# Attention on one core: transposes of the probabilities in pairs of units, with the value products behind them

## The reference

```python
scores = jnp.einsum('bsgqd,btgd->bgqst', q, k) * scale
scores = jnp.where(causal, scores, jnp.finfo(scores.dtype).min)
attn = jax.nn.softmax(scores, axis=-1)
out = jnp.einsum('bgqst,btgd->bsgqd', attn, v)
```

## Time and profile before

| | |
|---|---|
| median of the runs | 927.78 us |
| the profiled execution's time | 926.08 us |
| its span | 924.3 us |
| TensorE (PE) busy | 909.6 us, 98% |
| weight loads (PEld) busy | 804.3 us, 87% |
| VectorE (DVE) busy | 628.5 us, 68% |
| ScalarE (ACT) busy | 514.9 us, 56% |
| GpSimd (POOL) busy | 488.1 us, 53% |
| granted TensorE clock | 1.00 |

### The profile page before, as it was taken

The page is one execution under the profiler, slowest core; times in us unless marked ns, Lnnn a source line. Parts: engine busy times, 40 slices in busy tenths (PEclk is TensorE's granted clock), DMA queues, the critical chain, the costliest instruction groups (busy, mean ns, idle before and its releaser), DMA issues.

```text
span 924.3 us, 15010 instructions
## 1 busy us (share of the span) xinstructions
PE 909.6 (98%) x5480; PEld 804.3 (87%) x5480; DVE 628.5 (68%) x1297; ACT 514.9 (56%) x1121; POOL 488.1 (53%) x699
## 2 busy tenths in 40 slices
PE   6999999999999999999999999999999999999997
PEld 5889889888888898888888898888888998888886
DVE  6578668856786678647875787378757876764554
ACT  4376566745765566557664766476647667531111
POOL 1386638561866286708671867076717989410000
PEclk9999999999999999999999999999999999999999
DMA  8000100000001000000010000000001001000000
GB/s 284 1 24 1 40 1 24 1 29 1 24 1 40 1 23 1 29 1 23 2 41 1 24 1 29 2 1 24 1 1 69 1 14 62 1 23 0 23 23 23
DMA packets 10180, 21.21 MB, mean 23 GB/s; under 512 B 1280, under 2 KB 5760, under 8 KB 9984
## 3 DMA queue, kind: packets, MB, share of 16 engines
q1 hardware_dynamic: 9392, 20.11, 6.4%
q10 hardware_dynamic: 720, 0.21, 0.1%
HBM read 18.22 MB, written 2.10 MB: 22 GB/s over the span
## 4 chain that ended last, share of the span: by engine, by line
PE 94%; DVE 2%; ACT 2%; issue 1%; DMA 0%; SPq 0%; DVEq 0%; ACTq 0%
PE ps L1286 13%; PE ps L1129 13%; PE ps L1130 13%; PE ps L1131 13%; PE ps L1307 7%; PE ps L1304 7%; PE ps L1305 7%; PE ps L1269 7%; PE ps L1275 6%; PE ps L1272 6%; ACT prob L780 1%; PE ps L1153 1%; DVE ps L1042 1%; PE ps L1140 1%; PE ps L1265 1%
## 5 line engine op out<-in xcount | busy, mean ns | idle before, releaser
L625 POOL TENSOR_TENSOR rinv<-rsum,mone 128x1 f32<-128x1 f32 x256 | 140.9, 550 | 230.5 <-ACT prob L780 229.9
L1046 DVE TENSOR_TENSOR pt_lo<-ps,pt_hi 128x512 fp32r<-128x512 f32 x288 | 198.1, 688 | 64.6 <-ACT pt_hi L804 61.3
L804 ACT ACTIVATE pt_hi<-ps 128x512 fp32r<-128x512 f32 x288 | 171.2, 597 | 116.5 <-PE ps L1286 114.2
L780 ACT ACTIVATE prob<-ps,nmax 128x256 f32<-128x256 f32 (+28 forms) x256 | 180.7, 706 | 82.9 <-DVE nmax L1042 81.1
L630 POOL TENSOR_SCALAR prob<-prob,rinv 128x256 f32<-128x256 f32 (+28 forms) x256 | 190.2, 743 | 38.8 <-POOL rinv L625 38.5
L1042 DVE CUSTOM_DVE_ANT_0 ps<-ps,mask_f 128x256 f32<-128x256 f32 (+28 forms) x256 | 183.1, 718 | 38.6 <-PE ps L1275 33.0
L1286 PE MATMUL ps<-ident,prob 128*128 128x128 f32 x1152 | 172.6, 273 | 1.0 <-POOL prob L630 0.8
L1286 PEld LDWEIGHTS ps<-ident,prob 128*128 128x128 f32 x1152 | 140.4, 141 | 20.9 <-DVE pt_lo L1046 3.4
L1304 PE MATMUL ps<-pt_hi,v_hi 128*128 128x512 f32 x288 | 134.3, 466 | 0.0
L1307 PE MATMUL ps<-pt_lo,v_hi 128*128 128x512 f32 x288 | 114.1, 396 | 0.0
L1305 PE MATMUL ps<-pt_hi,v_lo 128*128 128x512 f32 x288 | 113.5, 394 | 0.0
(11 more groups left out here) (179 smaller groups left out, 1814.1 us busy)
## 6 DMA issues: line engine op xcount, KB each, us to landing
w_raw<-in_wqkv SPq DMA_DIRECT2D x8, 640.0 KB, 4.1
wp_raw<-in_wproj SPq DMA_DIRECT2D x8, 512.0 KB, 3.5
out_y<-prob SPq DMA_DIRECT2D x8, 256.0 KB, 2.3
x<-in_x SPq DMA_DIRECT2D x3, 512.0 KB, 12.2
prob<-in_wug SPq DMA_DIRECT2D x3, 512.0 KB, 4.1
prob<-in_wmod SPq DMA_DIRECT2D x1, 1024.0 KB, 9.6
wv_raw<-in_wv SPq DMA_DIRECT2D x4, 256.0 KB, 4.6
raw_down<-in_wdn SPq DMA_DIRECT2D x1, 1024.0 KB, 4.8
```

The costliest lines, as they stand in the source:

```text
L780: a_.activation(row(i, h).rearrange("p (a n) -> p a n", a=nb), score_banks(i, h).rearrange("p (a n) -> p a n", a=nb)[:, :, 0:w], ACT.Exp, ...
L1046: v_.tensor_tensor(pt_lo[:, n % 3, :], ring(t, "T", n), pt_hi[:, n % 3, :].bitcast(F32), ALU.subtract).then_inc(ptl_done, 1)
```

## The change

A function `together` rewrites the list after it is made. For each n of 4, 6, 8, ... up to 34 (in the last turn up to 26) it puts T(n-1), T(n), V(n-3), V(n-2) at the place of T(n-1), and all that stood between them behind, in its old order. ScalarE's copy `pt_hi` of units above 2 gets a wait for V(n-3), which reads the same slot.

```diff
-WALK = walk()
+def together(order):
+    for t in range(TURNS):
+        for n in range(4, NU if t + 1 < TURNS else LAST[WINDOWS[2][0]] + 1, 2):
+            first = order.index((t, "T", n - 1, 0))
+            stop = order.index((t, "V", n - 2, 0)) + 1
+            pair = [(t, "T", n - 1, 0), (t, "T", n, 0), (t, "V", n - 3, 0), (t, "V", n - 2, 0)]
+            rest = [item for item in order[first:stop] if item not in pair]
+            order[first:stop] = pair + rest
+    return order
+
+WALK = together(walk())
...
                 if what == "T":
                     act.wait_ge(t_done, this(t_done, t, n + 1))
+                    if n > 2:
+                        act.wait_ge(pv_done, this(pv_done, t, n - 2))
                     a_.activation(pt_hi[:, n % 3, :], ring(t, "T", n), ACT.Copy).then_inc(pth_done, 1)
```

## The result

The kernel after takes 963.35 us (median of five runs, 961.22 to 966.54), the kernel before beside it on the same chip 927.44 us (926.73 to 928.13): ratio 1.0393, 95% interval 1.038 to 1.0406. Forecast were 963 us and a range of 943 to 980. The profiled execution took 963.04 us with a span of 961.3 us, 37.0 us more than that of before. The five runs differ in their mean granted clock: the fastest, 961.22 us, has 1.000, the profiled one 0.998, and the three slowest 0.995.

What follows compares the result with a forecast made beforehand. TensorE was taken as the bound, with almost no gaps, and grouping as saving nothing. A 8, B 5, C 14 and D 8.4 make 35 us on the profiled 926.1, so 961; the median's 1.7 more gives 963, range 943 to 980.

Steps and rivals of the forecast that it cites:

- B: S5.3, each turn: waits for an exponential whose maximum stands behind LF; 0.6 us a turn, 5 us over eight turns.
- C: T15 and T16, each turn: T16 waits 1.6 us for the modulation; 1.75 us a turn, 14 us over eight turns.
- A: T4 and T6, each turn: they wait for pt_lo, 0.47 and 0.78 us; 8 us over eight turns.
- D: End of seven turns: S0.1 waits 0.8 us for S7.3's exponential; with smaller waits 1.2 us a turn, 8.4 us.
- rival 6: Around T16: the clock falls and T13 to V14 take up to twice as long; 56 us more, 1019 us; chance 0.02.
- Rival 2: All pairs: changing from transposes to products costs 0.09 us, which grouping saves, and waits are hidden; 917 us; chance 0.05.
- rival 3: All turns: the waits appear, but long steps behind them take each up; about 928 us, no change; chance 0.04.
- 4: All turns: only part of the waits appears, as ScalarE gets to pt_hi earlier; 930 to 943 us; chance 0.05.
- Rival 5: Whole turn: ScalarE falls behind and all pairs lose 0.4 us or more; over 980 us; chance 0.04.

Runs made afterwards that it cites:

- late_pairs: The kernel after with only the pairs n = 22 to 30 grouped, 38 in all: 928.76 us, ratio 1.0017 to the kernel before.
- apart_16: The kernel after with only the pair n = 16 (T15 and T16) left apart as before: 966.11 us, ratio 1.0427 to the kernel before.
- l_after_y1: The kernel after with the layer norm's transposes and what follows them moved behind Y1: 956.33 us, ratio 1.0327 to the kernel before.
- apart_34: The kernel after with only the pair n = 34 (T33 and T34) left apart as before: 954.44 us, ratio 1.0293 to the kernel before.
- four_slots: The kernel after with four slots for pt_hi and pt_lo and no new ScalarE wait in turns 0 to 6: 963.22 us, ratio 1.0382.
- cheap_pairs: First experiment: the kernel after with pairs n = 4, 6, 10, 16 and 34 left as before, 85 of 124 grouped: 961.83 us, ratio 1.0371.
- four_cures: The kernel after without pairs up to 8 and at 34, layer norm's transposes behind Y1, LF ahead of Y0, gates early: 932.35 us, ratio 1.0057.

## Why the prediction was right, point by point

The time was forecast within 0.4 us, and so near only by luck. B was 2.5 us too large and C 1.0, and T19 to T31 gave back 0.9 that was not forecast. Against that 3.3 us at turn 1's end and 0.8 in the last turn were missing, and 1.2 came from the clock at the start. The chains, the waits and their places were right.

**Bound and saving.** TensorE had no slack, and the 0.09 us ahead of a V's second matmul was no price of switching. `late_pairs` shows it: 38 pairs did not save the 3.4 us that it would have given.

**A** was right in place, cause and size: 0.50 and 0.75 us against 0.47 and 0.78, 8.3 us against 8.

**B** was right in its cause and mis-sized: 0.6 a turn became 0.2 to 0.3 (0.7 and 0.6 in the first and last turn), 2.5 us against 5. S5.3 did wait 0.6, but the walk forecast 1.05 and took LF's last instruction as long as in the earlier trace rows, then shaded by its median; in turn 2 it took 0.17. Less the 0.36 that S5.3 lost before, 0.25 is left.

**C** was right: 1.6 us of wait, 1.58 a turn beyond before, 13.0 against 14. In turn 2 the forecast waits of V12 and T15, 0.2 us each, are absent, and of the 0.25 to be taken off for before only 0.05 came off from T13 to T15, so two errors nearly cancel in the 1.75. That the modulation holds T16 is shown by `apart_16` and `l_after_y1`: 1.6 us fell to 0.3 and 0.1. Neither gave all of C back, since T18 then waited for `pt_lo`(16).

**D** was right: 1.23 a turn against 1.2, and `apart_34` gave 0.9 of it back.

**Missing terms.** The gates of turn 1: I worked D out in turn 2 and multiplied by seven, without a look at what else VectorE does in each turn. That is 3.3 us, the clock's share in it, some 1.1, included. I left the clock out because my longest wait was 1.6 us; for waits of that length this held, eight times at T16, at 1.00. The wait that I hadn't found, 3.1 us, stands ahead of the low clock in five traces. By the mean clocks (0.995 in three of the five runs, 0.998 in the profiled one, 1.000 in the fastest) the low clock took more of some runs and none of another; where, the one trace does not tell. So the median holds a clock loss that the forecast left out. The Trainium skill ("TensorE: Matmul & The Clock Gate", section "Part 4: PE-mode transpose") says that transposes don't count as busy time for the clock in the same way as matmuls; T15, 1.6 us of wait and T16 in a row left it at 1.00 here, so rival 6 did not occur at its place, and no run tells more of that rule. The last turn has fewer steps to cover a Y, 0.8 us.

**The other rivals.** Rival 2 (a price of switching) falls with `late_pairs`, rival 3 (hidden waits) and 4 (a part of them) with the lag, which never shrinks by more than 0.2 us in a turn. Rival 5 (ScalarE behind for the whole turn) fails twice: from T19 to T31 the lag is flat, and `four_slots` without the new wait has the same time.

**The wrong step behind it.** It was not in the prediction but in the first experiment's expectation: I took the other pairs for cheap in any company. Behind a single unit they are cheap only with enough work between: T22 lost 0.13 us in `late_pairs`, T12, T8 and T18 lost 0.5, 1.2 and 1.7 in `cheap_pairs`. What an edit of an order costs depends on the distance, in TensorE's work, between T(n) and T(n+2) after all edits. The time from one start to the other was 3.1 to 3.4 us in these waits on `pt_lo` behind an exponential or an `o_hi`: T4 to T6 3.40 in the kernel after, T6 to T8 3.15 and T10 to T12 3.11 in `cheap_pairs`, T16 to T18 3.31, 3.31 and 3.35. It is no constant: T20 to T22 in `late_pairs` is 2.56, with a wait too.

Left open are the causes of the 0.6 us a turn and of the last turn's 2.3 in `four_cures`, and why the clock fell at the start of `cheap_pairs`.

## What to carry to other kernels

In a kernel whose tensor engine is full, the cover behind which the other engines empty a buffer is worth more than a tidy order of its own instructions: for each step moved, add up the tensor work between the two uses of the same bank and hold it against the chain that empties it. Undo such an edit in whole or check what comes next: a single unit ahead of a pair could be as bad as the pair removed. A figure worked out in one turn should be multiplied only after a look at what is different in the others.

## What was not expected of the hardware

- The granted clock fell behind a wait of 3.1 us without matmuls (0.53 over the next 3.6 us, in five traces) and stayed at 1.00 behind 1.6 us. This cost some 1.1 us beside the wait itself. It also fell once with TensorE at work (0.51 over 3.5 us at the start of `cheap_pairs`).
- The length of a record misleads, start to start does not: the first matmul behind transposes reads 0.48 us against 0.39 and costs nothing more, as `late_pairs` shows.
- Changing from transposes to products and back costs TensorE at most 0.04 us here, by the lag in `late_pairs`.
